# TensorE signals by a drain behind its products instead of on the last product, in a two-layer graph network

## What is computed

```python
# layer 0, for all edges e = (src -> dst)
out_s = (x_s[src] * es) @ W_ss / 8 + (x_v[src] . ev) @ W_vv * ...
out_v = ...                                    # x_s[src] x ev, x_v[src] * es, through W_sv, W_vs
scale = sigmoid(edge_scalars @ W_rad.T + b_rad)     # 160 factors an edge: the "radial" part
h = x + segment_sum(concat(out_s, out_v) * scale, dst)
x = layernorm(x + linear(h))
# layer 1
w = silu(edge_scalars @ Wfc1) @ Wfc2           # 192 factors an edge, "hidden" and "radial" products
msgs = w * (features of x[src], edge harmonics)
n = segment_mean(msgs, dst)
x = layernorm(x + self_part(x) + (n_scal @ Wa) * linear(n))
```

## Time and profile before

| | before |
|---|---|
| median of 3 runs | 5404.95 us (5401.82 to 5424.09) |
| the profiled execution | 5458.66 us, span 5456.8 us |
| mean granted TensorE clock over the span | 0.739 |
| busy: TensorE products, weight loads | 4384.4 us (80%), 2659.6 us (49%) |
| busy: VectorE, ACT, POOL | 3868.2 us (71%), 2607.9 us (48%), 3314.4 us (61%) |
| layer 0's loop, layer 1's loop | 2587 us, 2597 us |

### The profile page before, as it was taken

How to read it: one execution, slowest core, us unless ns; L and a number is a source line. 1 busy time by engine, 2 the same in 40 slices (tenths; PEclk the granted TensorE clock), 3 DMA queues, 4 the chain that set the end, 5 groups by cost and what they waited for, 6 DMA issues and landing times.

```text
span 5456.8 us, 61361 instructions
## 1 busy us (share of the span) xinstructions
PE 4384.4 (80%) x12412; PEld 2659.6 (49%) x12413; DVE 3868.2 (71%) x8785; ACT 2607.9 (48%) x8195; POOL 3314.4 (61%) x3267
## 2 busy tenths in 40 slices
PE   6778677777777777777878988888888888888887
PEld 4555455555555455555644444444444444444445
DVE  4777777777777777776757666767666667667677
ACT  3444444444544545444544444444444444444444
POOL 4666666666666666666356666666666656666661
PEclk7555555555555555555788988999999989999898
DMA  7555555555555555555323223323322323223231
GB/s 241 154 155 158 148 155 153 149 154 155 155 153 155 147 154 158 152 156 151 102 80 83 81 77 83 82 80 82 81 81 80 82 76 83 81 80 81 79 83 52
DMA packets 245760, 640.14 MB, mean 117 GB/s; under 512 B 57085, under 2 KB 95407, under 8 KB 245627
## 3 DMA queue, kind: packets, MB, share of 16 engines
q0 software_dynamic: 181152, 556.66, 37.5%
q1 hardware_dynamic: 64576, 83.11, 5.1%
HBM read 618.66 MB, written 20.88 MB: 117 GB/s over the span
## 4 chain that ended last, share of the span: by engine, by line
DVE 33%; PE 29%; another core or an unknown queue 18%; issue 11%; ACT 5%; DVEq 3%; DMA 1%; ACTq 0%; POOL 0%; SPq 0%; POOLq 0%
PE ps L963 17%; DVE work L675 9%; DVE work L658 6%; DVE onehot L708 5%; PE ps L956 5%; ACT work L470 4%; PE ps L950 3%; PE ps L943 2%; DVE acc L715 2%; DVEq L772 1%; DVE work L653 1%; DVE work L663 1%; DVE work L664 1%; DVE work L695 1%
## 5 line engine op out<-in xcount | busy, mean ns | idle before, releaser
L373 POOL DMA_INDIRECT work<-table,srcs x1596 | 1633.9, 1024 | 936.5 <-issue 790.7
L373 POOL DMA_INDIRECT arena<-table,srcs x1596 | 1603.4, 1005 | 940.9 <-issue 893.2
L963 PE MATMUL ps<-arena,onehot 128*128 128x161 f32 x3608 | 1065.6, 475 | 643.3 <-DVE arena L681 532.7
L963 PE MATMUL ps<-work,onehot 128*128 128x384 f32 x3608 | 1381.2, 532 | 82.7 <-DVE work L702 64.9
L963 PEld LDWEIGHTS ps<-arena,onehot 128*128 128x128 f32 x3608 | 912.0, 317 | 970.3 <-issue 958.3
L470 ACT ACTIVATE work<-work,harm 128x96 f32<-128x96 f32 (+1 forms) x3224 | 1070.4, 416 | 24.9 <-DVE work L702 14.1
L470 ACT ACTIVATE work<-arena,harm 128x160 f32<-128x160 f32 (+1 forms) x3224 | 984.8, 389 | 96.5 <-DVE arena L681 77.9
L963 PEld LDWEIGHTS ps<-work,onehot 128*128 128x128 f32 x3608 | 702.3, 204 | 657.6 <-issue 305.9
L943 PE MATMUL ps<-wrad,escal 49*128 49x320 f32 x1612 | 918.7, 716 | 0.0
L956 PE MATMUL ps<-fc,hid 128*128 128x384 f32 x1612 | 656.3, 533 | 285.7 <-ACT hid L560 208.9
L498 ACT ACTIVATE ps<-ps 128x640 f32<-128x640 f32 x403 | 276.9, 687 | 1194.2 <-PE ps L943 534.7
(11 more groups left out here) (127 smaller groups left out, 2488.6 us busy)
## 6 DMA issues: line engine op xcount, KB each, us to landing
escal<-in_escal SPq DMA_DIRECT2D x404, 98.0 KB
arena<-table,srcs POOLq DMA_INDIRECT x1596
work<-table,srcs POOLq DMA_INDIRECT x1596
table<-work SPq DMA_DIRECT2D x49, 224.0 KB, 4.8
dst_sh<-in_dst_sh SPq DMA_DIRECT2D x52, 160.0 KB
table<-work SPq DMA_DIRECT2D x7, 784.0 KB, 4.0
acc<-in_xd SPq DMA_DIRECT2D x1, 3920.0 KB
arena<-in_xd SPq DMA_DIRECT2D x7, 560.0 KB, 4.2
```

What stands on the lines that cost most here:

```text
L373: pool.indirect_dma_start(out=rows[:, j, t, :], out_offset=None, in_=table, in_offset=bass.IndirectOffsetOnAxis(ap=of[:, j, t:t + 1], axis ...
L963: last = mm(bank(to)[:, 0:(MSG0, MSG1)[l]], onehot[:, b, t, :], m[:, j % 2, t, :], start=t == 0, stop=t == TPS - 1)
```

## The change

Three signals of TensorE move from the last product of a group to a drain instruction issued behind the group: layer 0's radial products (`s_lin[0]`) and the sums of both layers (`s_agg[0]`, `s_agg[1]`). A drain lets TensorE's stream go on only when the engine has finished what was issued before it, and then raises the semaphore. The sums of further windows (`s_aggx`), the hidden and radial products of layer 1 (`s_lin[1]`, `s_w2`) and everything outside the two loops keep their signals on products.

```diff
@@ -941,7 +941,7 @@
                 pe.wait_ge(s_esc[0][j // PAIR], (i + 1) * 16)
                 for k in range(2):
                     last = mm(rad[j % 2][:, 2 * k:2 * k + 2, :], escal[:, j, k * P:(k + 1) * P], wrad[:], start=True, stop=True)
-                last.then_inc(s_lin[0], 1)
+                pe.drain().then_inc(s_lin[0], 1)
 
             def hidden1(s, i, j):
 
@@ -979,7 +979,8 @@
                         with pe.Fori(1, more):
                             further()
 
-                sums(l, j, j % 2, FIRST + j % 2).then_inc(s_agg[l], 1)
+                sums(l, j, j % 2, FIRST + j % 2)
+                pe.drain().then_inc(s_agg[l], 1)
 
             def edge_layer(l):
                 visit = pe.alloc_register(f"further_visit_to_sum{l}")
```

## The result

The changed kernel takes **5673.28 us** (median of 4 runs, 5661.6 to 5686.68) against 5410.53 for the kernel before on the same chip: ratio 1.0484, 95% interval 1.0447 to 1.0521. It is 4.8% slower, where 5.6% faster was forecast, and lies above the range. The span of its profiled execution is 5659.8 us against 5456.8, so 203 us longer.

What follows compares the result with a forecast made beforehand. Late TensorE signals were taken to bound the kernel; with drains TensorE would. Gains of 150 us in layer 0 and 150 in layer 1, together 300, off the median 5404.95 gave 5105 us, range 4850 to 5560.

Steps and rivals of the forecast that it cites:

- What bounds the kernel: Both edge layers: signals attached to TensorE's products are at times held 4 to 8 us after the product.
- Cost of a drain: TensorE in both loops: drain signal about 0.05 us after products, restart 0.10 us behind sums, 0.31 behind radial products.
- 3.0 x 101 = 303 us: Layer 1: gain from 22.7 against 25.7 us a round, if no signal were held any more.
- the 150 us taken for each layer: Layer 0: gain of 1.5 us a round; layer 1: half of the span from nothing to 303 us.
- Rival 3: Both layers: the drain is held as well, TensorE's idle time stays on top; slower, 5960 us, chance 0.13.
- a round of 22.7 us: Layer 1 with drains and no holds: products 18.8, ended overlap and drains 1.7, loop end 0.8, further windows 1.4 us.
- 24.1: Layer 0's round in us with drains, TensorE bounding, against 25.6 before.
- 20.1 + 1.2: Layer 0, a round: 20.1 us for four groups each of sums and radial products, 1.2 for further windows.
- 1.6 + 0.8: Layer 0, a round: 1.6 us of TensorE restarts behind drains, 0.8 for the loop's end.
- Rival 5: Both layers: no signal matters, drains are pure cost, 3.4 and 2.5 us a round; 6005 us, chance 0.07.
- rival 2: Layer 0 is freed, layer 1 not, its unmoved signals held as before; 5305 to 5455, given as 5355 us, chance 0.15.

Runs made afterwards that it cites:

- run 3: The kernel before without the gathers inside the loops, signals on products: 4356.3 us, one run.
- run 4: The changed kernel, with its drains, without the gathers inside the loops: 4890.8 us, one run.
- run 2: The kernel before with drains in layer 0 alone, behind radial products and sums; layer 1 signals on products: 5500.12 us, ratio 1.0048.
- run 1: The kernel before with the drain behind layer 1's sums alone; layer 0 signals on products: 5740.85 us, ratio 1.0487.
- run 9: The kernel before without SP's loads of edge scalars inside the loops, gathers kept: 5375.5 us, one run.
- runs 5 and 6: Kernel before and changed kernel, each with POOL waiting behind every second supertile's gathers until they landed: 5603.11 and 5604.53 us, ratios 1.0237 and 1.0241.
- runs 7 and 8: Kernel before and changed kernel, POOL waiting for the previous supertile's landing behind every second supertile's first gather: 5279.74 and 5513.85 us, ratios 0.9623 and 1.0051.

## Why the prediction was wrong

**What bounds the kernel** was read rightly: signals of TensorE that come 4 to 8 us late are where a round's 5 us go. Counted over the trace of the kernel before, 127 of 403 sigmoids start more than 0.5 us after both their products' end and ACT's last work, 579 us together, and 145 of 403 silus, 608 us: 5.7 and 6.0 us a round. Without gathers (run 3) none and one do, and a round takes 20.3 and 20.0 us against 25.5 and 25.8.

**The step that failed** is the first of "Cost of a drain": "So a drain's own signal comes about 0.05 us after the products". It rests on one drain at 5440.4, which runs when no gather does. Prompt drains do follow in 0.02 us, but inside the loops 154 of 1209 were more than 0.5 us late. From that step came "3.0 x 101 = 303 us, if no signal were held any more" and the 150 us taken for each layer. TensorE's report is late whatever carries it, so moving the increment ended no hold; it moved it. The sigmoid's own signal is late 27 times in place of 127 (41 us in place of 579), but the drain behind the sums is late by 209.7 us, and TensorE stands still meanwhile. Whether the completion or the drain's own increment is held was not tried, since every drain carried one; that TensorE's stream stands until then speaks for the completion. **Rival 3**, given 0.13, is what happened.

**The drain's price without holds** was nearly right. Layer 1: a round of 22.7 us was worked out, run 4 shows 22.8. Layer 0: 24.1 against 22.8, and that two errors offset each other is luck. In run 4's trace the products with the further windows fill 19.0 us a round, where 20.1 + 1.2 were put: 103 of the 402 groups of radial products and 77 of the 355 single groups of sums took less than 2.0 us, many about 1.35, where 2.5 was taken for all, at a granted clock of 0.58 over the layer. TensorE stands 3.7 us between them, where 1.6 + 0.8 were put: the restart behind sums is 0.06 to 0.19 us and behind radial products mostly 0.46 (0.10 and 0.31 were taken), and 0.9 us is waiting for messages. Rival 5's difference, 3.4 and 2.5 us a round, measured 2.5 and 2.8.

**Layer by layer.** If all that the gathers add is put down to the holds (in layer 1 the clock, 1.00 in place of 0.91, is part of it), holds cost 25.5 - 20.3 = 5.2 and 25.8 - 20.0 = 5.8 us a round before. After, they cost 25.5 - 22.8 = 2.7 and 27.8 - 22.8 = 5.0. That agrees with the late drains counted in layer 0, (39.8 + 209.7)/101 = 2.5; in layer 1 the drains give 312.9/101 = 3.1, and the silu's unmoved signal was late besides ("remote" 239.5 us). So in layer 0 drains cost 2.5 us a round and the holds shrank by as much: forecast -150 us, measured -2 (run 2: +25). In layer 1 they cost 2.8 and the holds shrank by 0.8 only: forecast -150, measured +199 (run 1: +265). Why the holds shrank so differently isn't settled.

**Rival 3's size.** It put 6.4 and 3.6 us of holds on top of 24.1 and 22.7, and so 5960. Measured are 2.7 and 5.0 on 22.8 and 22.8. TensorE's idle time in the earlier trace rows was no measure of the holds: in layer 0 it waits for messages too, 162.5 us even without gathers (run 3). A slip besides: the middle of rival 2's 5305 to 5455 is 5380, not 5355, which changes nothing here.

**Rules of the Trainium skill.** The Trainium skill, "TensorE: Matmul & The Clock Gate", section "The cost: per-tile semaphore tail", has one increment on the last product as sound, and its figures give an estimate of about 56 ns for the tail. Run 3 agrees: with no gathers the sigmoid starts 37 ns after its products in the median, and the drains of run 4 cost 4891 - 4356 = 534 us. The kernel before, with its 127 late sigmoids, doesn't. Rival 2's rule, from the Trainium skill, "VectorE: DVE Perf Modes" (the section on the TRN2 errata: increments at a high rate from one engine can deadlock another, and dense ones from several should be spaced), is not settled. The drains that were held carried increments themselves, so they speak neither for it nor against it; run 9 shows only that SP's loads are no cause, and the increments of the gathers' landings were not varied.

**Where the bare price hides.** It is under POOL where POOL bounds: runs 5 and 6 are level. In layer 1 of runs 7 and 8, 27.2 against 25.0, price and holds are mixed and not told apart.

## What to carry to other kernels

A signal that comes late now and then isn't mended by another instruction to carry it before it is known what makes it late: look for what other engine's activity the late ones share, by counting over the trace, and then take that activity away, since the count alone can't tell cause from effect. A drain inside a loop costs TensorE its run ahead, here 2.5 to 2.8 us a round of four supertiles, and when it is held it holds the whole stream. Where POOL gathered without pause beside TensorE, two short waits of POOL a round for its own gathers to land were worth 3.8% with signals on products (run 7); longer ones cost more than the holds (run 5).

## What the hardware showed that was not expected

- While indirect gathers follow one another every 1.25 us, TensorE's work is reported late, products' and drains' alike: in the changed kernel 117 of 157 drains are late from the tenth gather on, against 36 of 962 with fewer gathers behind them, and without gathers 1 of 1209. No sharp count is shown: where POOL pauses after every eighth gather, 114 of the 357 drains behind the eighth are late, by 1.4 us on average over that run's late ones. The drains that come free in a pause do so 2.1 (layer 0) and 1.7 us (layer 1) after the last gather in the median.
- With signals on products a pause of 1.6 us or more between gathers ends the long holds in layer 0 of run 7, one of 1.2 to 1.3 us doesn't in layer 1.
- The hold doesn't depend on the gathers' bytes or rows: at a quarter of either it stayed. What of a gather does it, its instruction on POOL or the increments of its landing, and whether fewer and larger gather instructions would keep it away, wasn't tried and is open.
